# Linear attention by column quarters: when the state is taken, and where gamma and beta of the values come in

## The reference

```
qh = split_heads(layernorm(q @ wq) * gamma + beta)          # 56 rows a batch
kh = split_heads(layernorm(k @ wk) * gamma + beta)          # k = v = context, 1500 rows
vh = split_heads(layernorm(v @ wv) * gamma + beta)
q_prime = relu(qh) + 1e-6
k_prime = (relu(kh) + 1e-6) * mask;   vh = vh * mask
kv  = einsum('bhnd,bhne->bhde', k_prime, vh)                # 8 x 8 per head: the state
z   = 1 / (einsum('bhnd,bhd->bhn', q_prime, k_prime.sum(-2)) + 1e-6)
att = einsum('bhnd,bhde,bhn->bhne', q_prime, kv, z)
out = layernorm(att.reshape(b, -1, 128) @ dense_w + dense_b)
```

## Time and profile before

| | |
|---|---|
| median of 3 runs | 771.31 us |
| profiled execution, its own time | 770.22 us |
| its span | 768.4 us |
| busy over the span: PE, DVE, ACT, POOL | 671.1, 538.7, 510.4, 270.7 us |
| granted TensorE clock, mean | 0.962 |

### The profile page before, as it was taken

One profiled execution on the slowest core, in us unless ns is written; L12 is line 12 of the kernel. 1 busy time (PEld: TensorE's weight loads), 2 busy tenths in 40 slices (PEclk: granted clock), 3 DMA queues, 4 the chain that ended last, 5 costly groups with the idle time before them and its releaser, 6 DMA issues.

```text
span 768.4 us, 19268 instructions
## 1 busy us (share of the span) xinstructions
PE 671.1 (87%) x7283; PEld 469.5 (61%) x7283; DVE 538.7 (70%) x1252; ACT 510.4 (66%) x807; POOL 270.7 (35%) x324
## 2 busy tenths in 40 slices
PE   3599999997367899899999999999999988899997
PEld 3477777775124566566556666665666566467777
DVE  5799999998967887788778877878877761312122
ACT  4487777775425787787787777787788777443431
POOL 4398888883341132324314313313332110000000
PEclk9899999999668999999999999999999999799999
DMA  4122222253460763475376356537644671211110
GB/s 141 40 81 81 80 80 80 80 156 58 62 139 13 158 143 92 109 171 108 77 159 131 94 118 137 125 88 165 133 99 112 131 153 36 62 31 41 44 41 25
DMA packets 59379, 74.42 MB, mean 97 GB/s; under 512 B 35320, under 2 KB 40178, under 8 KB 59306
## 3 DMA queue, kind: packets, MB, share of 16 engines
q1 hardware_dynamic: 59306, 73.39, 40.4%
HBM read 32.35 MB, written 1.40 MB: 44 GB/s over the span
## 4 chain that ended last, share of the span: by engine, by line
PE 49%; DVE 9%; issue 7%; ACT 3%; POOL 2%; SPq 1%; DMA 1%; DVEq 0%; POOLq 0%; ACTq 0%
PE ps L741 9%; PE ps L654 8%; PE ps L814 7%; PE ps L802 7%; PE ps L728 6%; PE ps L646 4%; DVE mx L1584 4%; PE ps L640 4%; ACT P L992 1%; PE ps L676 1%; POOL KP L1101 1%; DVE silu L1499 1%; DMA QS<-QD 1%; SPq L442 1%; DVE QS L1590 1%
## 5 line engine op out<-in xcount | busy, mean ns | idle before, releaser
L992 ACT ACTIVATE P<-ps,kbias,kscale 125x896 f32<-125x896 f32 x192 | 210.3, 1098 | 92.8 <-PE ps L728 89.2
L1584 DVE TENSOR_REDUCE mx<-ps 128x1 f32<-128x500 f32 x336 | 215.6, 671 | 51.7 <-PE ps L654 49.0
L654 PE MATMUL ps<-KP,Qb 128*128 128x500 bf16 x336 | 129.0, 386 | 15.8 <-DVE mx L1584 7.1
L1101 POOL TENSOR_TENSOR KP<-kvall,KP 128x1500 bf16<-128x1500 f32 x16 | 48.6, 3040 | 226.1 <-ACT KP L935 226.1
L741 PE MATMUL ps<-P,Vp 125*32 125x112 f32 x3072 | 114.2, 266 | 1.4 <-ACT P L992 1.2
L741 PEld LDWEIGHTS ps<-P,Vp 125*32 125x32 f32 x3072 | 67.6, 109 | 48.7 <-issue 32.2
L531 PE MATMUL ps<-wkv,cT 128*125 128x256 f32 x384 | 91.9, 383 | 0.8 <-ACT arena L892 0.8
L531 PEld LDWEIGHTS ps<-wkv,cT 128*125 128x125 f32 x384 | 69.3, 190 | 9.9 <-issue 1.1
L728 PE MATMUL ps<-QS,KS 128*128 128x112 bf16 x768 | 70.1, 215 | 5.8 <-issue 4.3
L728 PE MATMUL ps<-QS,arena 128*128 128x112 bf16 x768 | 68.2, 215 | 6.9 <-issue 4.3
L728 PEld LDWEIGHTS ps<-QS,KS 128*128 128x128 bf16 x768 | 55.9, 99 | 28.9 <-issue 8.6
(11 more groups left out here) (213 smaller groups left out, 1017.4 us busy)
## 6 DMA issues: line engine op xcount, KB each, us to landing
cT<-ctxT_dram SPq DMA_DIRECT2D x32, 750.0 KB, 4.2
KS<-KP SPq DMA_DIRECT2D x48, 375.0 KB, 7.3
arena<-KP SPq DMA_DIRECT2D x48, 375.0 KB, 7.2
QS<-QD SPq DMA_DIRECT2D x96, 28.0 KB, 5.7
wgu<-w_dram SPq DMA_DIRECT2D x8, 256.0 KB, 3.1
silu<-w_dram SPq DMA_DIRECT2D x8, 256.0 KB, 3.0
x<-xh_dram SPq DMA_DIRECT2D x1, 512.0 KB, 3.6
mixed<-att SPq DMA_DIRECT2D x16, 28.0 KB
```

Source lines behind the costliest of these rows:

```text
L654: ins = nc.tensor.matmul(ps[:, bank, 0:KCW], q[:, 128 * c:128 * c + 128], KP[par][0][:, KCW * k:KCW * k + KCW], start=True, stop=True)
L992: nc.scalar.activation(P[t % 2][0:TK, :].rearrange("p (k n) -> p k n", k=2), src, ACT.Exp, scale=kscale[0:TK, bass.ds(n, 1)], bias=kbias[0 ...
L1101: nc.gpsimd.tensor_tensor(KP[par][2][:], krest, KP[par][1][:], ALU.subtract).then_inc(sem("kp3_ready"), 1)
L1584: ins = v.tensor_reduce(mx[:, c, k:k + 1], ps[:, bank, 0:KCW], AX.X, ALU.max)
```

## The change

1. **State by column quarters.** Each `kv_group` matmul is split into four. Quarter j takes 32 key columns against the 32 value columns of the same heads and the two factors, and writes 32 partitions of the bank, columns 0 to 33. The tile `VN` therefore holds the values as four quarters of 32 columns with the three factors behind each, and POOL writes the factors four times (48 elements per row for 12).
2. **State on DVE and ACT.** DVE multiplies the 34 columns by two small masks (`mquad`, `hquad`) into `kvc`, 40 columns wide. ACT (`expand`) copies each quarter of the partitions to its place in `kvall`, which POOL has set to zero at the start; `kvall` is 160 columns a batch.
3. **One group behind.** PE runs `y_group` of group n + 3 and then `kv_group` of group n - 1. The loops on PE and DVE write out one pair more.
4. **Gamma and beta on the numerators.** Gamma and beta of the values no longer enter the state. `normalise` multiplies the result by gamma and adds beta times the weighted sum of the mask (a second set of 16 columns from the numerators) times the reciprocal.
5. **relu with a stride.** The relu of the keys goes over its tile with the four context tiles innermost, at a step of 128 elements, in place of a contiguous run.

The core of the diff:

```diff
 SLOTS = 2 * NG
-KVW = D + H
+KVW = D + 2 * H
+QUAD = 32
+NQ = D // QUAD
+HQD = H // NQ
+BLK = QUAD + 2 * HQD
+VB = QUAD + 3
 EPS_LN, EPS_IN = 1e-5, 1e-6
...
                 for t in range(GT):
-                    ins = nc.tensor.matmul(ps[:, 6 + par, 0:D + 2], KN[0:TK, s6, t, :], VN[0:TK, s6, t, 0:D + 2],
-                                           start=(g == 0 and t == 0), stop=(g == NG - 1 and t == GT - 1))
+                    for j in range(NQ):
+                        r = QUAD * j
+                        ins = nc.tensor.matmul(ps[r:r + QUAD, 6 + par, 0:QUAD + 2], KN[0:TK, s6, t, r:r + QUAD],
+                                               VN[0:TK, s6, t, j, 0:QUAD + 2], start=(g == 0 and t == 0),
+                                               stop=(g == NG - 1 and t == GT - 1), skip_group_check=True)
                 ins.then_inc(sem("kv_done"), 1)
...
             def numerators(batches):
+                pe.wait_ge(sem("kv_put"), batches[-1] + 1)
                 for b in batches:
...
             def pair(i):
-                first = isinstance(i, int) and i == 0
-                last = isinstance(i, int) and i == B // 2 - 1
+                first, second, last = (isinstance(i, int) and i == k for k in (0, 1, B // 2 - 1))
                 for g in range(NG):
                     y_group(2 * i + 1, 1, g, False)
-                    kv_group(2 * i, 0, g, first)
+                    if g > 0:
+                        kv_group(2 * i, 0, g - 1, first)
+                    elif not first:
+                        kv_group(2 * i - 1, 1, NG - 1, second)
                 for g in range(NG):
...
                         y_group(2 * i + 2, 0, g, False)
-                    kv_group(2 * i + 1, 1, g, first)
-                    if last and g == 1:
-                        numerators(range(0, 4))
+                    if g > 0:
+                        kv_group(2 * i + 1, 1, g - 1, first)
+                    else:
+                        kv_group(2 * i, 0, NG - 1, first)
+                if last:
+                    numerators(range(0, 4))
+                    kv_group(2 * i + 1, 1, NG - 1, False)
...
                     c0 = 1024 * (k % NG) + 256 * t + D
-                    ins = nc.scalar.activation(VN[0:TK, k, t, 0:D], ps2[0:TK, c0:c0 + D], ACT.Copy,
-                                               scale=VN[0:TK, k, t, D + 2:D + 3])
+                    ins = nc.scalar.activation(VN[0:TK, k, t, :, 0:QUAD],
+                                               ps2[0:TK, c0:c0 + D].rearrange("p (j d) -> p j d", j=NQ), ACT.Copy,
+                                               scale=VN[0:TK, k, t, 0, QUAD + 2:QUAD + 3])
                 ins.then_inc(sem("vn_ready"), 1)
+            def expand(b, par):
+                act.wait_ge(sem("kv_read"), b + 1)
+                for j in range(NQ):
+                    r = QUAD * j
+                    ins = nc.scalar.copy(kvall[r:r + QUAD, bass.ds(b, 1), BLK * j:BLK * j + BLK],
+                                         kvc[r:r + QUAD, par, :].unsqueeze(1))
+                ins.then_inc(sem("kv_put"), 1)
...
                         deviation(n, k)
+                        if g == 1 and not first:
+                            expand(2 * i + par - 2, par)
+            act.wait_ge(sem("kv_zeroed"), 1)
             in_pairs(act, pair, B // 2)
             values(NG * B - 1, SLOTS - 1)
+            expand(B - 2, 0)
+            expand(B - 1, 1)
             act.wait_ge(sem("setup_in"), 80)
...
             ins.then_inc(sem("filled"), 1)
+            nc.gpsimd.memset(kvall[:], 0.0).then_inc(sem("kv_zeroed"), 1)
...
                 pool.wait_ge(sem("rk_ready"), n + 1)
-                nc.gpsimd.tensor_tensor(VN[0:TK, k, :, D:D + 3], emcat[0:TK, bass.ds(b * T + GT * g, GT), :],
-                                        rk[0:TK, k % 2, :, 1:4], ALU.mult).then_inc(sem("emc_ready"), 1)
+                nc.gpsimd.tensor_tensor(VN[0:TK, k, :, :, QUAD:VB],
+                                        bc(emcat[0:TK, bass.ds(b * T + GT * g, GT), :], 2, [TK, GT, NQ, 3]),
+                                        bc(rk[0:TK, k % 2, :, 1:4], 2, [TK, GT, NQ, 3]),
+                                        ALU.mult).then_inc(sem("emc_ready"), 1)
                 pool.wait_ge(sem("kn_ready"), n + 1)
...
             v.tensor_copy(emcat[0:TK, :, 1], em[0:TK, :]).then_inc(sem("em_ready"), 1)
-            hm3 = bc(hmask[:], 2, [128, H, DK])
-            v.tensor_tensor(gmask[:].rearrange("p (h d) -> p h d", h=H),
-                            row[:, GAMMA, :].rearrange("p (h d) -> p h d", h=H), hm3, ALU.mult)
-            step(v.tensor_tensor(bmask[:].rearrange("p (h d) -> p h d", h=H),
-                                 row[:, BETA, :].rearrange("p (h d) -> p h d", h=H), hm3, ALU.mult))
+            step(v.tensor_reduce(hquad[:], hmask[:].rearrange("p (j h) -> p h j", j=NQ), AX.X, ALU.add))
+            step(v.tensor_copy(mquad[:].rearrange("p (h d) -> p h d", h=HQD), bc(hquad[:], 2, [128, HQD, DK])))
             dve.wait_ge(sem("q0_ps"), 1)
...
                 dve.wait_ge(sem("kb0_ready"), n + 1)
-                kn = KN[0:TK, k, :, :]
+                kn = KN[0:TK, k, :, :].rearrange("p t d -> p d t")
                 v.tensor_scalar(kn, kn, 0.0, EPS_IN, ALU.max, ALU.add).then_inc(sem("kp_ready"), 1)
-            def state(b, par):
+            def state(b, par, first_pair=False):
                 dve.wait_ge(sem("kv_done"), NG * (b + 1) + SLOTS)
+                if not first_pair:
+                    dve.wait_ge(sem("kv_put"), b - 1)
                 kv = ps[:, 6 + par, :]
-                v.tensor_tensor(kvtmp[:, par, :], kv[:, 0:D], gmask[:], ALU.mult).then_inc(sem("kvt_ready"), 1)
-                v.tensor_tensor(kvall[:, bass.ds(b, 1), D:KVW], hmask[:].unsqueeze(1),
-                                bc(kv[:, D + 1:D + 2], 1, [128, 1, H]), ALU.mult)
-                dve.wait_ge(sem("kvt_ready"), b + 1)
-                v.scalar_tensor_tensor(kvall[:, bass.ds(b, 1), 0:D], bmask[:].unsqueeze(1), kv[:, D:D + 1],
-                                       kvtmp[:, par, :].unsqueeze(1), ALU.mult, ALU.add).then_inc(sem("kv_read"), 1)
+                v.tensor_tensor(kvc[:, par, 0:QUAD], kv[:, 0:QUAD], mquad[:], ALU.mult)
+                v.tensor_tensor(kvc[:, par, QUAD:BLK].rearrange("p (k h) -> p k h", k=2), bc(hquad[:], 1, [128, 2, HQD]),
+                                bc(kv[:, QUAD:QUAD + 2], 2, [128, 2, HQD]), ALU.mult).then_inc(sem("kv_read"), 1)
                 bank, c = nd_place(t)
-                return ps[:, bank, c:c + KVW]
+                return ps[:, bank, c:c + KVW].rearrange("p (j n) -> p j n", j=NQ)
             def normalise(tiles):
+                lo, hi = tiles[0], tiles[-1] + 1
+                n = hi - lo
+                quads = lambda ap: ap.rearrange("p (j h) -> p j h", j=NQ)
                 for t in tiles:
-                    ins = v.tensor_scalar(xn[:, t, 0:H], nd(t)[:, D:KVW], EPS_IN, None, ALU.add)
+                    ins = v.tensor_scalar(quads(xn[:, t, 0:H]), nd(t)[:, :, QUAD + HQD:BLK], EPS_IN, None, ALU.add)
                 step(ins)
-                lo, hi = tiles[0], tiles[-1] + 1
                 step(v.reciprocal(xn[:, lo:hi, H:2 * H], xn[:, lo:hi, 0:H]))
                 for t in tiles:
-                    ins = v.tensor_tensor(att[:, t, :].rearrange("p (h d) -> p h d", h=H),
-                                          nd(t)[:, 0:D].rearrange("p (h d) -> p h d", h=H),
-                                          bc(xn[:, t, H:2 * H], 2, [128, H, DK]), ALU.mult)
-                ins.then_inc(sem("att0_ready"), 1)
+                    v.tensor_tensor(quads(xn[:, t, 2 * H:3 * H]), nd(t)[:, :, QUAD:QUAD + HQD], quads(xn[:, t, H:2 * H]),
+                                    ALU.mult)
+                    ins = v.tensor_tensor(att[:, t, :].rearrange("p (j h d) -> p j h d", j=NQ, d=DK),
+                                          nd(t)[:, :, 0:QUAD].rearrange("p j (h d) -> p j h d", d=DK),
+                                          bc(quads(xn[:, t, H:2 * H]), 3, [128, NQ, HQD, DK]), ALU.mult)
+                step(ins)
+                for t in tiles:
+                    v.tensor_tensor(att[:, t, :], att[:, t, :], row[:, GAMMA, :], ALU.mult)
+                    ins = v.tensor_tensor(t0[:, t, :].rearrange("p (h d) -> p h d", h=H),
+                                          row[:, BETA, :].rearrange("p (h d) -> p h d", h=H),
+                                          bc(xn[:, t, 2 * H:3 * H], 2, [128, H, DK]), ALU.mult)
+                step(ins)
+                v.tensor_tensor(att[:, lo:hi, :], att[:, lo:hi, :], t0[:, lo:hi, :], ALU.add).then_inc(sem("att0_ready"), 1)
```

More of the change, by code:

```diff
@@ L263, in build @@
         kvall = sb("kvall", [128, B, KVW])
-        kvtmp = sb("kvtmp", [128, 2, D])
+        kvc = sb("kvc", [128, 2, BLK])
+        mquad = sb("mquad", [128, QUAD])
+        hquad = sb("hquad", [128, HQD])
         ss = sb("ss", [128, 2, 2 * GT])
@@ L267, in build @@
```

(41 more changed lines are left out.)

## The result

The changed kernel takes 790.24 us in the median of 4 runs (789.32 to 790.38), the kernel before 770.78: a ratio of 1.0247, 95% interval 1.0229 to 1.0265. It is slower; 765.6 was forecast. All ratios are of fast runs; one run of 2734.43 us, of the kernel with gamma and beta back in the state, is thus not in its ratio. The profiled execution took 789.32 us with a span of 787.5, 19.1 more than before.

What follows compares the result with a forecast made beforehand. DVE's state work held the stage at 3.116 us per group; POOL would then set 2.87. Over 45 groups -11.1, end +5.35: -5.75 on 770.22 gives 764.5, plus 1.09 for the median 765.6; range 760 to 777 us.

Steps and rivals of the forecast that it cites:

- The sum: Whole kernel: 45 groups at 2.87 us instead of 3.116 give -11.1, the end +5.35, together -5.75 us.
- The step on the stride: Relu on DVE with a 512-byte step: 0.42, 0.69 or 1.22 us possible, 0.6 taken; DVE stays at 2.6 per group.
- the nearest row: Profile row of copies of 192 elements written at a 12-byte step, 0.26 to 0.30 us; basis for the relu's 0.6.
- the penalty: Trainium skill's rule: accesses that each fall on another 16-byte line of SBUF are penalised; the prediction set it aside.
- the first branch: Strided relu stays in pairs, holds the way into SBUF 0.27 us longer per group, and POOL goes to 3.14.
- the second rival: The relu's 512-byte step halves its rate, slowing POOL or DVE; at 3.17 per group 779.4 us, slower; chance 0.18.
- The step on ACT: Four state copies per batch on ACT, 0.8 us taken; ACT's idle 2.2 us per batch hides them on average.
- The third rival: ACT's copies hold the next square; POOL waits 0.23 per group, pace 3.1, 776 us; chance 0.09.
- The end: Stage's end on DVE, gamma and beta in the normalisations: +1.2 and +4.15, together +5.35 us, without a gap.
- The state on DVE: Two masked multiplies per batch on DVE, of 32 and 8 elements: 0.3 us in place of 1.29.
- The factor multiply: POOL's multiply grows from 12 to 48 elements: 0.08 us more than 0.21; POOL's pace 2.82 to 2.89.
- PE was no bound: State matmuls as 32 short records: 0.32 to 1.04 us, 0.85 taken; PE needs 2.67 per group; rival chance 0.16.

Runs made afterwards that it cites:

- 767.4: The changed kernel with a contiguous relu and ACT's four copies moved behind the next square, ahead of its values: 767.36 us, ratio 0.9958.
- 762.2: The changed kernel with contiguous relu, gamma and beta back in the state, and ACT's copies behind the next square: 762.17 us, ratio 0.9894.

## Why the prediction was wrong

**The sum.** Forecast for the profiled span was 768.4 - 5.75 = 762.65; it is 787.5, 24.85 more. The pace is 3.355 in place of 2.87, over 45 groups 21.8. The last group, from its multiply to the end of the add, took 3.65 for 2.98: 0.7. The end took 6.73 for 5.35: 1.4. About 1.0 comes behind the second normalisation, and its cause stays open.

**The step on the stride failed.** "I take 0.6, near today's median, since the copies are the nearest row", the prediction says, and also that their step "can neither confirm nor refute" the penalty. The second is so: their 12 bytes lie between the 8 that cost nothing and the 16 that cost, and the relu's 512 lie beyond both. With POOL idle it takes 0.71 us, close to the 0.69 that I had worked out and not taken. On DVE that is 0.1 per group more than I took, and by the forecast's own sum DVE would still have been below POOL. It matters on POOL, whose add beside it goes from 1.34 to 1.52 and stands still for longer. That fits pairs kept at half rate: one element at a time, the sum of two tensors at this step took 1.15. This is the first branch of the second rival, which put POOL at 3.14 (3.07 came). The rule of the Trainium skill that I set against this part (Advanced Engine Details and Errata, section Memory Cachelines) agrees with these runs: two accesses to a 16-byte line cost nothing (0.43 at a step of 8 bytes), one access to a line is penalised (0.63 at 16). I gave it 0.18.

**The step on ACT failed.** Its size was right: 0.91 us for four copies, 0.8 taken. "Which hides it on average" was the mistake. Most of ACT's idle time lies ahead of the values, where it waits for POOL and DVE (27.9 us over the span of the kernel before); the copies stood ahead of the square, where it had only 5.5. The square late by 0.9 delays DVE, and DVE's relu then misses the moment between two POOL instructions and waits out a whole add of 1.27. The third rival put this at 0.23 per group and named the square, the reduction and POOL; the two runs that differ only in the place of the copies show 0.31, and idle copies at that place the same. That the relu would make it worse by missing its moment was not in the prediction.

**The rivals were priced one at a time.** Each alone would have come out a little above my range's upper end of 777 (777.8 with the copies moved, 781.6 with the relu contiguous). Both came, and they add; the text had no case for that.

**The end.** The DVE work was sized rightly. Removing gamma and beta took 5.46 us off the stretch from POOL's last add to the second normalisation's end, in the two runs of 767.4 and 762.2 (15.18 and 9.72), for 5.35 forecast. The rest is a wait that I had excluded ("DVE goes on without a gap"): 1.48 us for the numerators. On PE the key projections ahead of them took 2.04 for 1.10 and they 2.79 for 1.69, at the granted clocks of 0.50 and 0.65. That the 24 numerator records are 160 columns wide in place of 144 cannot be it: at 144 columns, in the kernel of 762.2, they took 2.96 at 0.55.

**What was right.** The state on DVE takes 0.25 us per batch (68.94 to 69.19), 0.3 forecast. The factor multiply takes 0.27 for 0.285. POOL becomes what sets the pace, at 2.88 per group, once the two mistakes are taken out: the kernel of 767.4 has that pace and all else of the change. DVE has less in hand than forecast: busy for 38.88 of 40 us there, 2.80 per group, where I took 2.6. PE was no bound; 32 short records take 0.46 us, near the lower end of 0.32 to 1.04, not at the 0.85 that I took. The zeroing and the order on PE cost nothing that the runs can show.

## What to carry to other kernels

An engine's idle time is no cover for new work unless it lies at the place where the work is put: look which wait follows it in the engine's order, and put it in front of a wait that is there anyway. Here 0.9 us of work in the wrong place cost 0.94 us in every batch. Where an instruction has to fit between two of another engine, as the relu between POOL's, it has a phase as well as a duration: 0.06 us behind the start of POOL's add it took 1.81 us, one group earlier 1.13. When two rivals act on different instructions of one cycle, price the case in which both come.

## What the runs showed of the hardware that was not expected

- DVE's scalar operation on 512 elements: 0.43 us up to a step of 8 bytes, 0.62 to 0.74 from 16 bytes on; a sum of two tensors at 512 bytes 1.15.
- Four column quarters of 32 x 34 make a stream of 32 matmul records in 0.46 us, 14 ns each.
- A PE that is idle more often ran the stage at a granted clock of 1.00 (27.61 of 40 us busy), but got 0.66 in the stage's end, where 0.93 stood before. The lower of the two levels, 1.2 GHz, shows in the last row of PE above: eight value projections take 2.07 us at a granted clock of 0.50, in the kernel of 762.2 the same eight take 1.14 at 1.00. PE had stood idle for 3.98 us a little before, while DVE normalised, against 0.81 there.
- Ahead of the numerators the clock is down by 188.43: 32 products take 0.68 us there and 0.46 in the stage, and PE had stood idle for 3.96 us. Whether that idle time lowered it was not tried.
